# A decoder on one core: query and key biases as columns in ScalarE's copies, and a new order of GpSimd's work at the heads of both attention runs

## The chip, the cores and the metric

One core of a Trainium2 chip runs the whole program. The metric is the time of one execution in microseconds, the median of several. Five engines work beside each other in it: TensorE (PE in the profile; its weight loads are PEld), VectorE (DVE), ScalarE (ACT), GpSimd (POOL) and SyncE (SP), which here only issues DMAs. Each runs its own list of instructions in order and waits on semaphores.

## The reference, cut to what matters

The input x is four batches (B = 4) of 256 rows of 128 numbers. It passes through two layers of a decoder. Layer 0 is self-attention with random features (16 heads of width 8), cross-attention with a second input ctx, and a routed feed-forward part; layer 1 is causal self-attention, cross-attention and a feed-forward part with product keys. Each attention starts with a layer norm. What the change touches are the projections of layer 0:

```python
q = layernorm(x) @ Wq.T + bq        # layer 0, self-attention: stage 0
k = layernorm(x) @ Wk.T + bk
v = layernorm(x) @ Wv.T + bv
qh = split_heads(q @ wq.T + bq)     # layer 0, cross-attention: stage 1, q from x, k and v from ctx
kh = split_heads(k @ wk.T + bk)
vh = split_heads(v @ wv.T + bv)
```

The causal attention of layer 1 (stage 2) has no biases, and its cross-attention (stage 3) has one only on the output.

## The kernel before, in words

A turn n is one batch of one stage: n = 0 to 3 are stage 0, 4 to 7 stage 1, 8 to 11 stage 2, 12 to 15 stage 3. For every turn `norm` (L885, VectorE) takes the moments of two tiles of 128 rows, GpSimd raises the variance to the power of -0.5 (`power`, L472), and VectorE scales (L904). TensorE then turns the result (`pre_x`, L1326), ScalarE copies it out (`evac_x`), TensorE multiplies by the query and key weights (`pre_qk`, L1308) and by the value weights (`pre_v`), and ScalarE copies these out (`evac_qk`, L663, one instruction for queries and keys together, and `evac_v`). The queries and keys lie with features on partitions, so that a bias is one number for each partition.

The biases are added on TensorE: `project` follows a product by one whose contraction has only three rows (L1313 for queries and keys, L1314 for the rest). The three rows are the bias split into three bf16 parts, which VectorE makes in `split_bias` (L259 to L273): for 512 columns ahead of the first product, and for the other 640 in three pieces at the end of the steps n = 0, 1, 2 of stage 0's loop.

Stage 0 has two loops: one over the four turns that makes features (L972 on VectorE), and one that combines keys and values and ends a turn with `onorm_rf`, `tail_b`, `resid`, and `norm` and `pre` of turns 4 and 5 (L1025). After it stages 1, and later 2 with 3, are run by `run(first, last)`, a list that each engine has for itself: `run(4, 7)` and `run(8, 15)`. A run has a head: scores by rows for all 16 heads of the first turn, whose maxima VectorE takes (L943; L940 and L941 in stage 2), `max_parts`, `max_turn` (L1457), three early score products of the next turn, and then a loop of scores by columns (L1429, behind L1425 in stage 2), exponentials (L705) and values. The places of the later turns' `pre_x`, `pre_qk` and `pre_v` in that loop come from `pres_at`. In the head `norm(first + 2)` stands between `max_parts` and the early row maxima, and its `pre_x` and `pre_qk` stand behind the first two of the loop's score products.

For each turn of a run GpSimd splits the queries and keys into three bf16 parts (`split`, L484 to L500), and SyncE places them by 12 DMAs (`place`, L412) into one of three stacks, which GpSimd must have cleared (`clear`, L517, a memset of 128 by 4096). Ahead of `place` stands `fixed`, which waits for that clear.

Between the two runs lies the routed feed-forward part: 32 leaves, each with rows gathered by GpSimd's DMAs, 16 dot products on VectorE (`hidden`, L1130, both inputs in SBUF), 16 scalings on ScalarE (L817, after L807) and 34 products on TensorE (L1685). `add_leaf` (L1139) adds the leaves 24 to 31 to x. Its last steps also do `norm` and `pre` of the turns 8 and 9: VECTOR_AT, TENSOR_AT and SCALAR_AT name the leaf before which each stands. On GpSimd turn 8's power stands behind the gathers of leaf 30 and turn 9's behind those of leaf 31; then come `split(8)`, `clear(2)`, `split(9)`, `clear(0)`, `clear(1)` and the power of turn 10. The stacks share their memory with the leaves' rings, so the clears wait for the leaves.

## Time and profile before

| | us |
|---|---|
| median of 3 runs | 813.09 (812.82 to 814.02) |
| profiled execution | 818.24 |
| its span | 816.5 |
| stage 0 | 0 to 115 |
| run of stage 1 | 115 to 220 |
| routed feed-forward part | 220 to 450 |
| runs of stages 2 and 3 | 450 to 620 |
| product keys | 620 to 816 |

The stages are read from the order of the instructions in the timeline; their borders are rounded. A line of the timeline gives the start and the duration in us, the engine, the source line and the operation, what it writes and reads, and in brackets how long the engine had been idle and what ended that.

### The profile page before, as it was taken

Reading aid. Unit: us, or ns where it says so; the run is one execution under the profiler, and the core shown is the slowest. Engines: PE = TensorE matmul, PEld = TensorE weight load, DVE = VectorE, ACT = ScalarE, POOL = GpSimd, SP = SyncE. Lnnn points to the kernel's source line nnn. Section 1 sums busy time; section 2 is a strip of 40 time slices with the busy share of each in tenths; the row PEclk is TensorE's granted clock in tenths of the full one; section 3 lists DMA queues with packets and bytes.
Section 4 is the critical chain, followed back from the end, with each engine's and each line's share of the span. In section 5 each row is a group of like instructions: output and inputs, shape, how many; then the busy total and the mean of one; then the engine's idle time right before and its main releaser. Section 6 shows DMA issues by size and latency. Waiting matters only on the chain. (4 is left out here: it accounts for less than half of the span.)

```text
span 816.5 us, 14593 instructions
## 1 busy us (share of the span) xinstructions
PE 678.3 (83%) x4864; PEld 513.5 (63%) x4864; DVE 598.5 (73%) x2443; ACT 440.3 (54%) x1054; POOL 320.7 (39%) x315
## 2 busy tenths in 40 slices
PE   3987987978767989989879379989987698888888
PEld 1556634535346677878769256665545488888888
DVE  5695556774468999998758277787735699999984
ACT  1224002646227887879988035556664665555562
POOL 3050052460143423233213622223001688888883
PEclk9985555989859999989999689999999899999999
DMA  7000020200088999999634212112000000000000
GB/s 241 2 1 3 1 80 16 58 14 2 1 328 312 358 366 386 346 357 413 235 134 183 72 37 59 44 43 58 26 3 0 1 2 5 4 4 5 5 4 7
DMA packets 38914, 86.07 MB, mean 105 GB/s; under 512 B 3985, under 2 KB 30129, under 8 KB 30647
## 3 DMA queue, kind: packets, MB, share of 16 engines
q0 software_dynamic: 9216, 69.47, 21.8%
q1 hardware_dynamic: 29622, 15.66, 6.7%
q8 instruction: 39, 0.64, 0.3%
q14 instruction: 37, 0.30, 0.1%
HBM read 74.42 MB, written 0.52 MB: 92 GB/s over the span
## 5 line engine op out<-in xcount | busy, mean ns | idle before, releaser
L817 ACT ACTIVATE arena<-arena,hact 128x128 f32<-128x128 f32 x512 | 155.5, 388 | 1.0
L705 ACT ACTIVATE arena<-psum 128x512 f32<-128x512 f32 (+1 forms) x192 | 101.5, 561 | 56.5 <-PE psum L1429 55.9
L606 POOL TENSOR_TENSOR arena<-arena 128x1024 f32<-128x1024 f32 x64 | 121.2, 1913 | 21.9 <-DVE arena L1269 16.4
L1130 DVE CUSTOM_DVE_ANT_0 arena<-arena,fx 128x128 f32<-128x128 f32 x384 | 106.1, 344 | 10.4 <-DMA arena<-tab_q,leaf_no 8.5
L863 ACT ACTIVATE psum<-arena,tneg 128x1024 f32<-128x1024 f32 x64 | 71.5, 1118 | 61.8 <-DVE arena L1269 29.1
L1793 PE MATMUL psum<-arena 128*128 128x128 f32 x688 | 91.1, 294 | 16.3 <-DVE arena L1269 10.0
L943 DVE TENSOR_REDUCE rowmax<-psum 128x2 f32<-128x512 f32 x128 | 81.5, 686 | 26.1 <-PE psum L1411 24.5
L1793 PEld LDWEIGHTS psum<-arena 128*128 128x128 f32 x688 | 87.6, 209 | 18.4 <-DVE arena L1269 11.1
L1685 PE MATMUL psum<-identf,arena 128*128 128x128 f32 x544 | 78.5, 301 | 16.0 <-ACT arena L817 15.2
L1685 PEld LDWEIGHTS psum<-identf,arena 128*128 128x128 f32 x544 | 71.3, 210 | 23.3 <-ACT arena L817 16.5
L1411 PE MATMUL psum<-arena 128*128 128x256 bf16 (+1 forms) x384 | 77.3, 296 | 10.2 <-DVE rowmax L943 9.6
L1685 PE MATMUL psum<-arena,identf 128*128 128x128 f32 x544 | 73.3, 288 | 5.1 <-ACT arena L817 4.6
L1685 PEld LDWEIGHTS psum<-arena,identf 128*128 128x128 f32 x544 | 67.1, 199 | 11.0 <-ACT arena L817 5.0
L1429 PE MATMUL psum<-arena 128*128 128x256 bf16 (+1 forms) x384 | 69.2, 275 | 4.0 <-DMA arena<-mt 2.4
L1269 DVE SCALAR_TENSOR_TENSOR arena<-arena,vaug,psum 128x1024 f32<-128x1024 f32 x43 | 54.5, 1273 | 15.2 <-ACT psum L863 13.0
L475 POOL TENSOR_TENSOR rstd<-var_e,halves 128x2 f32<-128x2 f32 x16 | 11.3, 705 | 130.6 <-DVE var_e L899 130.6
L1411 PEld LDWEIGHTS psum<-arena 128*128 128x128 bf16 x384 | 35.2, 105 | 32.4 <-DVE rowmax L943 26.5
L648 ACT ACTIVATE arena<-psum 128x128 f32<-128x128 f32 (+3 forms) x57 | 29.3, 514 | 47.0 <-PE psum L1445 10.4
L1445 PE MATMUL psum<-arena,vaug 128*32 128x256 f32 (+1 forms) x768 | 49.2, 375 | 1.9 <-ACT arena L705 1.9
L1429 PEld LDWEIGHTS psum<-arena 128*128 128x128 bf16 x384 | 33.7, 100 | 25.8 <-ACT arena L705 13.7
L1793 PE MATMUL psum<-arena,picked 128*128 128x128 f32 x336 | 44.6, 289 | 6.1 <-DVE picked L1269 6.1
L1793 PEld LDWEIGHTS psum<-arena,picked 128*128 128x128 f32 x336 | 42.3, 204 | 7.2 <-DVE picked L1269 7.1
(230 smaller groups left out, 1202.4 us busy)
## 6 DMA issues: line engine op xcount, KB each, us to landing
arena<-parts SPq DMA_DIRECT2D x144, 64.0 KB
w_sb<-attn_w SPq DMA_DIRECT2D x1, 768.0 KB, 7.9
x<-x_in SPq DMA_DIRECT2D x1, 512.0 KB, 4.1
fx<-ctx_in SPq DMA_DIRECT2D x1, 512.0 KB, 4.6
picked<-mask_in SPq DMA_DIRECT2D x1, 512.0 KB, 6.2
wq_sb<-peer_wq SPq DMA_DIRECT2D x1, 512.0 KB, 8.3
down_sb<-table_down SPq DMA_DIRECT2D x1, 512.0 KB, 9.5
up_sb<-table_up SPq DMA_DIRECT2D x1, 512.0 KB, 8.9
```

Source lines behind the costliest of these rows:

```text
L606: nc.gpsimd.tensor_tensor(grid[k % 3].rearrange("p (i j) -> p i j", i=PK), sim[:, t, h, :].unsqueeze(2).to_broadcast([P, PK, PK]), sim[:, ...
L705: nc.scalar.activation(probs[k % (2 * HG)][:, 0:w], bank(2 + k % 2, 0, w), ACT.Exp, scale=float(D) ** -0.5).then_inc(probs_ready, 1)
L817: a = nc.scalar.activation(w, w, ACT.Copy, scale=hact[i % 2][:, l:l + 1])
L863: nc.scalar.activation(psum[:, (4 + 2 * (k % 2)) * BANK:(6 + 2 * (k % 2)) * BANK], grid[k % 3], ACT.Exp, bias=tneg[:, t, h:h + 1]).then_in ...
L943: i = nc.vector.tensor_reduce(rowmax[n % 2][:, :, h], bank(k % 2).rearrange("p (s n) -> p s n", s=SUB), AX.X, ALU.max)
L1130: i = nc.vector.tensor_tensor_reduce(w, w, src, 1.0, r[:, LW * E + l:LW * E + l + 1], ALU.mult, ALU.add, hid[g % 4][:, l:l + 1])
L1269: nc.vector.scalar_tensor_tensor(out=picked[k % 3], in0=grid[k % 3], scalar=top[t][:, h, TOPK - 1:TOPK], in1=psum[:, (4 + 2 * (k % 2)) * B ...
L1411: i = nc.tensor.matmul(o[:, r:r + keys], q[:, s * P:s * P + P], kk[:, 0:keys], start=not causal, stop=True, skip_group_check=causal)
L1429: i = nc.tensor.matmul(bank(2 + k % 2, c * S, c * S + S - q0), kk[:, c * P:c * P + P], q[:, q0:S], start=not causal, stop=True, skip_group ...
L1445: i = nc.tensor.matmul(o, vaug[n % 4][:, c, g * HG + j, :], probs[(k + j) % (2 * HG)][:, c * S:c * S + S - q0], start=(c == 0), stop=(c == ...
L1685: i = nc.tensor.matmul(o, *ab, start=(l == 0), stop=(l == LW and f < 3))
L1793: i = nc.tensor.matmul(psum[:, o:o + P], picked[k % 3][:, c * P:c * P + P], diag[t % 2][:, h, :], start=(h == 0 and c % 4 == 0), stop=(h = ...
```

## The change: what it does

The query and key biases of stages 0 and 1 come in as a tile of 9 rows by 128 by one more DMA, are turned into columns by one TensorE transpose, and are copied out by two small ScalarE instructions. `evac_qk` then is two instructions in these stages, each with function Identity and a bias column; there are no three-row products for queries and keys, and `split_bias` makes 640 of 1152 columns. In the head of a run `norm(first + 2)` is done before the run (in stage 0's second loop, and behind the last leaf), and its `pre_x` and `pre_qk` stand ahead of the first score product by columns. On GpSimd `power(6)` stands ahead of `split(5)`; at the second head `split(8)` no longer waits behind turn 9's power, turn 9's and 10's powers stand behind `clear(2)`, and `split(9)` stands last.

```diff
         bias_p = sb("bias_p", [3, NB], bf16)
+        bias_c = sb("bias_c", [P, 6])
         nodes_sb = sb("nodes_sb", [P, 4, NODES])
...
+        bias_r = arena[0:9, 2048:2048 + P]
         bias_sb, bias_w = arena[0:3, 0:9 * P], arena[0:3, 9 * P:9 * P + 9 * P // 2].bitcast(bf16)
...
         nbias_ready = sem("nbias_ready")
+        bias_ps, columns_ready = sem("bias_ps"), sem("columns_ready")
         bias_ready, osb_ready, or_ps = sem("bias_ready"), sem("osb_ready"), sem("or_ps")
...
-            now = [("x", n + 2)] * (n in (B, 2 * B) and h == 0) + [("qk", n + 2)] * (n in (B, 2 * B) and h == 1)
-            now += [("v", n + 2)] * (h == 2) + [("x", n + 3)] * (h == H - 2) + [("qk", n + 3)] * (h == H - 1)
+            now = [("v", n + 2)] * (h == 2) + [("x", n + 3)] * (h == H - 2) + [("qk", n + 3)] * (h == H - 1)
             return [(what, m) for what, m in now if m <= last]
...
                      ("weigh", 2): 24, ("attend", 2): 25, ("route_f", 2): 25, ("weigh", 3): 27, ("attend", 3): 28,
-                     ("route_f", 3): 29, ("next", NEXT[0]): 29, ("next", NEXT[1]): 32}
+                     ("route_f", 3): 29, ("next", NEXT[0]): 29, ("moments", NEXT[1]): 31, ("scale", NEXT[1]): 32,
+                     ("next", NEXT[1] + 1): 32}
...
             sp.dma_start(w_sb[:, 0:4, :], attn_w[0:4].rearrange("a i o -> i a o")).then_inc(in_w, 16)
+            sp.dma_start(bias_r, attn_bias.rearrange("(a p) -> a p", p=P)).then_inc(in_w, 16)
             sp.dma_start(bias_sb, attn_bias.partition_broadcast(3)).then_inc(in_w, 16)
...
                                                  bass.IndirectOffsetOnAxis(no, 0)).then_inc(rows2_in[g % RING2], 16)
-                    if g >= len(ORDER) - SUB:
-                        power(NEXT[g - len(ORDER)])
+                    if g == len(ORDER) - SUB:
+                        power(NEXT[0])
                 split(NEXT[0])
...
                 clear(NEXT[0] % 3)
-                split(NEXT[1])
+                power(NEXT[1])
+                power(NEXT[1] + 1)
                 pool.wait_ge(leaf_done, len(ORDER) - 1)
...
                 clear((NEXT[1] + 1) % 3)
-                power(NEXT[1] + 1)
+                split(NEXT[1])
...
             clear(0)
+            power(B + 2)
             split(B + 1)
-            power(B + 2)
             run(*RUNS[0])
...
                     act.wait_ge(dd_ps, min(n - 1, B))
-                scale = float(D) ** -0.25 if stage(n) == 0 else 1.0
-                nc.scalar.activation(qk_f[n % 2][:, :, :], bank(5).rearrange("p (w n) -> p w n", w=2),
-                                     ACT.Copy, scale=scale).then_inc(qk_ready, 1)
+                if stage(n) < 2:
+                    act.wait_ge(columns_ready, 1)
+                    for w in range(2):
+                        i = nc.scalar.activation(qk_f[n % 2][:, w, :], bank(5, w * S, w * S + S), ACT.Identity,
+                                                 bias=bias_c[:, 4 * stage(n) + w:4 * stage(n) + w + 1],
+                                                 scale=float(D) ** -0.25 if stage(n) == 0 else 1.0)
+                    i.then_inc(qk_ready, 1)
+                else:
+                    copy(qk_f[n % 2][:, :, :], bank(5).rearrange("p (w n) -> p w n", w=2), qk_ready)
...
+            act.wait_ge(bias_ps, 1)
+            nc.scalar.activation(bias_c[:, 0:2], bank(6, 0, 2), ACT.Copy, scale=float(D) ** -0.25)
+            copy(bias_c[:, 4:6], bank(6, 4, 6), columns_ready)
             evac_x(0)
...
                 evac_mt(first)
+                evac_x(first + 2)
+                evac_qk(first + 2)
                 for n in range(first, last + 1):
...
-            def norm(n):
+            def moments_of(n):
...
                 nc.vector.tensor_scalar(var_e[:, :], mv[:, :, 1], 1e-5, None, ALU.add).then_inc(var_ready, 1)
+
+            def norm_scale(n):
+
+                b = batch(n)
                 dve.wait_ge(rstd_ready, n + 1)
...
                 dve.wait_ge(xn_ready, n + 1)
+
+            def norm(n):
+                moments_of(n)
+                norm_scale(n)
...
             dve.wait_ge(consts, 1)
-            dve.wait_ge(in_w, 48)
-            split_bias(nc.vector, link, 0, 4 * P)
-            nc.vector.tensor_copy(bias_w[:, 0:1], bias_p[:, 0:1]).then_inc(bias_ready, 1)
+            dve.wait_ge(in_w, 64)
+            split_bias(nc.vector, link, 2 * P, 4 * P)
+            nc.vector.tensor_copy(bias_w[:, 0:1], bias_p[:, 2 * P:2 * P + 1]).then_inc(bias_ready, 1)
             nc.vector.tensor_tensor(feat_w[:, :, :], head16[:, :].unsqueeze(2).to_broadcast([P, H, M]),
...
                 dve.wait_ge(zk_ready, n + 1)
-                if n < B - 1:
+                if 0 < n < B - 1:
                     split_bias(nc.vector, link, (4 + 2 * n) * P, min(6 + 2 * n, 9) * P)
-            nc.vector.tensor_copy(bias_w[:, 0:1], bias_p[:, 0:1]).then_inc(bias_ready, 1)
+            nc.vector.tensor_copy(bias_w[:, 0:1], bias_p[:, 2 * P:2 * P + 1]).then_inc(bias_ready, 1)
             link(nc.vector.tensor_reduce(kmax1[:, :], kmax[:, :], AX.X, ALU.max))
...
                     resid(n - 1)
-                if 1 <= n < B - 1:
+                if n >= 1:
                     norm(B + n - 1)
...
                 max_parts(first)
-                norm(first + 2)
                 for h in range(EARLY):
...
                             add_leaf(i - 2)
+                    elif what == "moments":
+                        moments_of(i)
+                    elif what == "scale":
+                        norm_scale(i)
                     elif what == "norm":
...
-            BIAS = {(0, 0): 0, (0, 1): 1, (0, 2): 2, (0, 3): 3, (1, 0): 4, (1, 1): 5, (1, 2): 6, (1, 3): 7, (3, 3): 8}
-
-            def project(o, lhs, rhs, key, by_row):
+            BIAS = {(0, 2): 2, (0, 3): 3, (1, 2): 6, (1, 3): 7, (3, 3): 8}
+
+            def project(o, lhs, rhs, key):
...
                 bias = bias_of(r * P, r * P + P)
-                if by_row:
-                    return nc.tensor.matmul(o, bias, ones[0:3, :], start=False, stop=True)
                 return nc.tensor.matmul(o, ones[0:3, 0:P], bias, start=False, stop=True)
...
                 for w, src in ((0, xn_t[n % 2][:, :]), (1, kv_of(n))):
-                    i = project(bank(5, w * S, w * S + S), w_sb[:, 4 * a + w, :], src, (a, w), True)
+                    i = project(bank(5, w * S, w * S + S), w_sb[:, 4 * a + w, :], src, (a, w))
                 i.then_inc(qk_ps, 1)
...
                     i = project(bank(4, S + s * P, S + s * P + P), kv[:, s * P:s * P + P], w_sb[:, 4 * a + 2, :],
-                                (a, 2), False)
+                                (a, 2))
                 i.then_inc(v_ps, 1)
...
                     i = project(bank(tail_bank(n) + 1, s * P, s * P + P), o[:, s * P:s * P + P], w_sb[:, 4 * stage(n) + 3, :],
-                                (stage(n), 3), False)
+                                (stage(n), 3))
                 i.then_inc(y_ps, 1)
...
             pe.wait_ge(consts, 1)
-            pe.wait_ge(in_w, 48)
+            pe.wait_ge(in_w, 64)
+            nc.tensor.transpose(bank(6, 0, 9), bias_r, identf[0:9, 0:9]).then_inc(bias_ps, 1)
             pre_x(0)
+            pre_qk(0)
             pe.wait_ge(bias_ready, 1)
-            pre_qk(0)
             pre_v(0)
...
                 max_turn(first)
+                pre_x(first + 2)
                 for h in range(EARLY):
                     score_rows(first + 1, h)
+                pre_qk(first + 2)
                 for n in range(first, last + 1):
```

## Rows read from the trace of the kernel before

**Rows 1.** The page's first part: engine, busy us, share of the span, instructions.
```profile
PE 678.3 (83%) x4864; PEld 513.5 (63%) x4864; DVE 598.5 (73%) x2443; ACT 440.3 (54%) x1054; POOL 320.7 (39%) x315
```

**Rows 2.** The timeline of the first 20 us: bias split, first projections, first features.
```profile
9.65 0.41 DVE L262 CAST arena<-arena 3x512 bf16<-3x512 f32 x1
...
14.60 1.22 PE L1308 MATMUL psum<-xn_t,w_sb 128*128 128x256 f32 x2 [4.18 <-DVE arena L969]
...
15.75 0.39 PE L1313 MATMUL psum<-ones,bias_p 3*128 3x256 bf16 x1
...
17.66 0.60 ACT L663 ACTIVATE qk_f<-psum 128x512 f32<-128x512 f32 x1 [6.81 <-PE psum L1313]
...
19.43 3.78 PE L1476 MATMUL psum<-feat_w,qk_f 128*128 128x512 f32 x4
```

**Rows 3.** ScalarE's groups by shape: busy us, mean ns of one, idle before.
```profile
L648 ACT ACTIVATE vaug<-psum 128x256 f32<-128x256 f32 x16 | 6.1, 384 | 13.9 <-PE psum L1314 9.2 <-PE psum L1308 4.8
```

**Rows 4.** The timeline of stage 0's first loop.
```profile
28.79 0.70 PE L1308 MATMUL psum<-xn_t,w_sb 128*128 128x256 f32 x2 [0.47 <-ACT xn_t L648]
...
31.25 1.04 POOL L482 TENSOR_TENSOR sq<-qk_f 128x512 f32<-128x512 f32 x1 [11.22 <-ACT qk_f L663]
...
31.38 1.19 DVE L265 TENSOR_TENSOR arena<-arena 3x256 f32<-3x256 f32 x1
...
33.42 0.41 DVE L265 TENSOR_TENSOR arena<-arena 3x256 f32<-3x256 f32 x1
...
48.09 0.60 DVE L904 TENSOR_SCALAR xn<-x,mv,rstd 128x128 f32<-128x128 f32 x2 [0.81 <-POOL rstd L475]
...
48.74 0.44 PE L1326 MATMUL psum<-identf,xn 128*128 128x128 f32 x2 [2.00 <-DVE xn L904]
```

**Rows 5.** The timeline at the end of the third turn of that loop.
```profile
54.84 7.06 DVE L266 CAST arena<-arena 3x128 bf16<-3x128 f32 x1
54.86 6.96 POOL L517 MEMSET arena<- 128x4096 f32 x2
...
63.39 1.23 DVE L982 TENSOR_REDUCE stab<-psum 128x32 f32<-128x1024 f32 x1
```

**Rows 6.** The timeline of stage 0's end and the first head.
```profile
98.94 0.39 PE L1313 MATMUL psum<-ones,bias_p 3*128 3x256 bf16 x1
...
127.79 0.41 PE L1457 MATMUL psum<-identb,mparts 128*48 128x128 bf16 x2 [1.88 <-DVE mparts L957]
...
131.68 0.64 PE L1429 MATMUL psum<-arena 128*128 128x256 bf16 x2
...
137.03 0.61 PE L1429 MATMUL psum<-arena 128*128 128x256 bf16 x2
```

**Rows 7.** The timeline from the last leaves to the second head.
```profile
431.57 5.08 PE L1685 MATMUL psum<-arena,identf 128*128 128x128 f32 x34
...
432.93 0.22 ACT L807 ACTIVATE hact<-hid 128x16 f32<-128x16 f32 x1 [0.72 <-DVE hid L1130]
...
443.48 0.72 POOL L475 TENSOR_TENSOR rstd<-var_e,halves 128x2 f32<-128x2 f32 x1 [13.33 <-DVE var_e L899]
444.18 0.60 POOL L495 CAST parts<-qk_f 128x512 bf16<-128x512 f32 x1
444.24 1.86 DVE L904 TENSOR_SCALAR xn<-x,mv,rstd 128x128 f32<-128x128 f32 x2 [0.84 <-POOL rstd L475]
...
455.80 6.96 POOL L517 MEMSET arena<- 128x4096 f32 x2
...
462.57 0.39 PE L1406 MATMUL psum<-causal_q,identb 128*128 128x256 bf16 x1 [10.83 <-DMA arena<-parts]
```

**Rows 8.** The timeline in the second head: ScalarE's table load.
```profile
475.30 1.28 ACT L705 ACT_TABLE_LOAD   x1
```

**Rows 9.** Busy us of each engine in two stretches, with TensorE's granted clock.
```profile
28.00:48.00 20.00, 17.36 (x77) 9.82 (x75) 17.20 (x39) 7.01 (x12) 3.41 (x4) 1.00 0.00 1
72.00:90.00 18.00, 18.00 (x100) 15.19 (x98) 8.51 (x14) 5.28 (x7) 0.00 (x0) 0.50 0.02 4
```

## The prediction

> **What bounds the kernel now.** I read the page first. No engine is full: TensorE is the busiest with 83% of the span [rows 1], so time is lost where one engine waits for another, and a change pays only at such places. The chain of waits reaches back only to the product keys and shows nothing of the three places that are changed, so I went through the timeline at each of them. In the first 20 us TensorE stands idle for 4.18 us until VectorE has split the biases; its first projection starts at 14.60 [rows 2]. In stage 0's first loop VectorE is as full as TensorE, and TensorE waits 2.00 us for turn 3's norm [rows 4]. At the end of the third turn a cast of VectorE takes 7.06 us and ends right behind two memsets of GpSimd (54.86 + 6.96 = 61.82), and the next row maximum starts only at 63.39 [rows 5]. At the second head TensorE is idle for 10.83 us until the parts of turn 8 lie in the stack [rows 7]. Everything behind such a place is carried by semaphores and would move with it.
>
> **Part A, the first projections.** TensorE no longer waits for the split. The scaled x is read out by about 10.9; I add 0.2 for the transpose of the bias tile and the two small copies in front of it. The first product then starts at 11.1 instead of 14.60. Each bias product lengthens its pair: from 14.60 to the next pair behind 15.75 lie 1.47 us where the pair itself takes 1.22, so 0.25 each at this speed [rows 2]. Queries and keys: 11.1 + 2 x 1.22 = 13.5. The values take the 1.9 us from the release of ScalarE's copy, 0.1 ahead of 17.66, to 19.43 [rows 2], and end at 15.4, if their own bias is there by 13.5. It is: the split begins at 9.65 as before, is half as wide, and its nine operations take some 3.4 us at the width of 256. The features start at 15.4 instead of 19.43: **-4.0**. ScalarE's copy becomes two of 256 columns, 0.38 each by the nearest row [rows 3] against 0.60 for one, so 0.16 more (up to 0.4, as a bias column may cost something); the features wait for the value products anyway, which covers it. The DMA of 4.6 KB is one more issue of 0.4 us in front of the others; if its landing is late, A loses up to 0.5.
>
> **Part B, stage 0's first loop.** VectorE's split behind turn 0 goes, some 3.9 us with the operation that takes 1.19 instead of 0.41 beside GpSimd's squares [rows 4]. So far it sat in front of turn 2's norm and turn 1's maximum. Followed step by step with durations of this trace, turn 2's scaling ends at about 29.4, the features of turn 1 at 29.3 (the maximum follows them, not the norm), turn 1's last subtraction at 35, the split of the next 256 columns at 39, turn 3's norm at 41.8. Before, that norm ended at 48.69 [rows 4]: -6.9, of which A gave 4.0. TensorE is through with turn 1's work by 41.8 as well, so its wait of 2.00 us goes and nothing takes its place. What is late next is the cast beside the memsets. Both chains, the split of 128 columns on VectorE and the clears on GpSimd, start from turn 3's norm: the clears came 6.8 us behind its start, the blocked cast at the same time [rows 4, 5]. After the change the one chain loses two bias products (0.28 at this speed) and gains 0.16 on ScalarE, the other loses nothing. So I let the stall stay, and it ends when the clears do, 6.8 earlier. A and B together: **-6.8**, between -4.8 (TensorE reaches its full speed only at the same absolute time as before, near 28, and 4 us of its work take twice as long) and -13.4 (the stall goes, a rival below).
>
> **Part C, stage 0's end.** TensorE works without a gap from 72 to 90 at half clock [rows 9] and nearly so to 115. Two turns lose two bias products each at 0.25: **-1.0** (0 to -1.3, with 0.32 by [rows 6] for the whole step). Turn 6's norm moves here, 1.3 us of moments and 0.6 of scaling on VectorE. It is hidden in VectorE's idle time of 7.1 us ahead of the last residual; GpSimd's power for it stands behind `clear(0)` and ahead of `split(5)`, which has about 1.5 us of idle time in front of it. Without that cover `split(5)` would be late by 0.7, and its DMAs have 10 us of row maxima before they are needed.
>
> **Part D, the first head.** Between `max_turn` (127.79) and the third score product by columns (137.03) lie 9.24 us [rows 6]. In the new order: 0.34 for `max_turn`, 0.55 for `pre_x`, 1.05 for two early products, then the third, which waits for a row maximum that is no longer behind the norm (until 2.8), two projections of 1.22 (5.3), two pairs of products as before (7.5). **-1.8**, of which 0.5 are bias products. The first product by columns comes later than before (5.3 against 3.89), so ScalarE starts later but then isn't interrupted; if that counts, D is +1.4, if nothing counts, 0. I take -1.7. Turn 7, in the loop, loses two bias products at 0.14: **-0.3**.
>
> **Part E, the second head.** GpSimd was held at turn 9's power until 443.48; `split(8)` followed at 444.18, and `clear(2)`, which SyncE needs ahead of its 12 DMAs, only then [rows 7]. Now `split(8)` runs at 431.6, when turn 8's projections are out, and the clear at 436.8, when TensorE is through with leaf 28 (431.57 + 5.08) [rows 7]. SyncE's 8 us of DMAs are over by 452, and TensorE's wait of 10.83 us would go. Three things are late in its place.
> First, `split(8)` reads SBUF for 3.5 us (0.60 + 1.16 + 0.61 + 1.16) while VectorE makes `hidden(29)`, for which ScalarE already waits 0.72 us [rows 7]. A VectorE operation with two SBUF inputs took 1.19 instead of 0.41 beside GpSimd [rows 4]. I take the same for `hidden`, though no row shows it: +3.5 on the leaves (0 to 3.5).
> Second, turn 9's moments ahead of `hidden(31)` are 1.4 us on VectorE, against a slack of 0.8: +0.7. The last leaf ends at 453.5 instead of 449.3, and TensorE is through with turn 9 at 456.1.
> Third, turn 10's scaling. It waits for a power behind which GpSimd starts `clear(0)` and `clear(1)` at once, 6.96 us [rows 7]. GpSimd won that race before: power, cast at 444.18, and the scaling took 1.86 instead of 0.60 [rows 4, 7]; and a cast waited through both memsets [rows 5]. So the scaling waits from 450 to 457, then beside `split(9)` to 458.8, and behind it on VectorE stand the last two `add_leaf` and all row maxima of turn 8. TensorE gets two heads further and waits. The maxima start at 459.3 instead of 463.3: **-4.0**. `split(9)` is late (457), but its DMAs are placed by 467, and turn 9's first scores are wanted at 471. In the head itself the order of part D is worth less, since ScalarE's table load of 1.28 [rows 8] was hidden behind the DMA of the maxima and now follows `evac_qk`: **-0.3** (+1 to -1.6). Bounds of E: -10.8 with neither block, -0.4 if `hidden` also waits 3.5 for `clear(2)`, a memset (and +0.6 with the worst of the head).
> The Trainium skill, SBUF — State Buffer, Who interferes with whom, speaks on that last bound: a VectorE instruction with two SBUF inputs contends with a GpSimd instruction that reads SBUF and not with one that only writes. By it the split blocks `hidden` and the memset doesn't, which is E as summed; E would be near nothing if it weren't so. No row of this trace has such an instruction beside a memset.
>
> **The sum.** -6.8 - 1.0 - 1.7 - 0.3 - 4.3 = -14.1. The profiled execution of 818.24 would become 804.1. The median of the runs is 5.15 lower, a difference that the change doesn't touch: 813.09 - 14.1 = **799.0**.
>
> **The rivals.**
> 1. The stall at the clears goes. It needs VectorE's last split (2.4 us) to be over before GpSimd's clears start, so that TensorE must be 1.5 us late behind turn 3's norm. Turn 3's maximum then comes 6.9 earlier, but the reduction over partitions waits for the clears: -6.6 more, 792.4. For it: the two chains meet within 0.02 us in the trace [rows 5]. Against it: both hang on one norm.
> 2. `hidden` isn't blocked by the split: the last leaf ends 3.5 earlier, and so do norm and clears: 799.0 - 3.6 = 795.4. For it: no row shows `hidden` blocked. Against it: its two inputs.
> 3. The second head gives nothing, because VectorE's blocks (split, clear and scaling) fill the 10.83 us: 799.0 + 4.3 = 803.3.
> 4. TensorE doesn't get its full clock in the first loop. For it: from 72 to 90 it is busy all the time and has 0.50 granted [rows 9]. In 20 us from 28 it is busy 17.36 at 1.00; at the speed of the prologue's pairs (1.22 us against 0.70 [rows 2, 4]) that is 12 more, and B's 2.8 go too: 799.0 + 14.8 = 813.8, no change within what can be measured.
> 5. Slower: Identity isn't in the table set that Exp uses. ScalarE then loads tables ahead of each of the eight changed `evac_qk` and again ahead of the next Exp: 16 x 1.28 = 20.5 [rows 8], all of it between a projection and what waits for it or in front of the exponentials, so 799.0 + 20.5 = 819.5. It decides from 11 loads on the path. Against it: Copy stands among the Exps without a load. The Trainium skill, ScalarE: Activation LUTs, Table sets: the hidden batching unit, counts identity among the functions that are in every set; by it this rival falls.
> A change that does nothing is not among them: the wait for the split is taken away in the code.
>
> **How the numbers follow.** The forecast 52%, its own range 795 to 803; rival 1 14%, rival 2 13%, rival 3 11%, rival 4 4%, rival 5 6%. The range takes in rivals 1 to 3 with some of their sums and leaves out 4 and 5: 789 to 808. Faster by over 0.2% (1.6 us, about what a measurement of this kernel can tell from no change): the first four, with little taken off, 0.88. Within 0.2%: 0.04. Slower: 0.08.
>
> **What would show it.** A: L1308 first at 11.1, L1476 first at 15.4. B: turn 3's L904 at 41.2 and no wait of TensorE behind it; the L266 of about 7 us still there, and L982 at 56.6. D: 7.5 us from `max_turn` to the third L1429. E: L495 of turn 8 near 422 (431.6 less A to D), L1130 with gaps of 0.6 and 1.2 beside it, L904 of turn 10 as long as two memsets, L1406 without a wait for the DMA. The prediction is wrong if ScalarE's table loads are more than seven, if the granted clock of the first 50 us differs, or if the leaves take longer by more than 5 us.

## The result, and the profile after

| | before | after |
|---|---|---|
| median of the runs | 813.10 (812.82 to 814.02) | 788.34 (785.38 to 789.27) |
| profiled execution | 818.24 | 788.61 |
| its span | 816.5 | 786.9 |

The ratio is 0.9687 (95% interval 0.966 to 0.9714): 24.8 us less. The forecast was 799.0, in a range of 789 to 808. The sign was right, the gain was 10.7 us larger than forecast, and the median lies 0.7 us below the range.

The first two parts of the page of after, to be read beside [rows 1]. TensorE has 16 us less busy time: the products are hardly fewer, but fewer of them run at half clock.

```profile
PE 662.3 (84%) x4849; PEld 506.1 (64%) x4849; DVE 603.8 (77%) x2434; ACT 442.1 (56%) x1064; POOL 321.1 (41%) x315
...
PEclk9985559898568999999999999999999899999999
```

The timeline of after from the first projection on [rows 2]. The four projection products are one unbroken group of 2.07 us, and turn 0's features start at 14.99 instead of 19.43. The half norms behind them take 1.01, and the next four products of the features 1.96.

```profile
10.82 2.07 PE L1335 MATMUL psum<-xn_t,w_sb 128*128 128x256 f32 x4 [0.47 <-ACT xn_t L653]
13.11 0.80 PE L1335 MATMUL psum<-w_sb,xn_t 128*128 128x128 f32 x2 [0.22 <-DVE arena L993]
14.99 3.78 PE L1502 MATMUL psum<-feat_w,qk_f 128*128 128x512 f32 x4
18.57 1.01 PE L1513 MATMUL psum<-half,sq 128*128 128x16 f32 x8
19.43 1.96 PE L1502 MATMUL psum<-feat_w,qk_f 128*128 128x512 f32 x4
```

The end of the third turn of after, GpSimd's row first [rows 5]. The two memsets still hold VectorE's casts, but as two waits of 3.26 and 2.81 with two operations between them, and turn 3's row maximum (L1006, before L982) follows at 52.19 instead of 63.39.

```profile
44.52 7.04 POOL L521 MEMSET arena<- 128x4096 f32 x2
...
44.84 3.26 DVE L269 CAST arena<-arena 3x128 bf16<-3x128 f32 x1
48.13 0.34 DVE L273 SCALAR_TENSOR_TENSOR bias_p<-arena,identf,bias_p 3x128 bf16<-3x128 bf16 x1
48.51 0.28 DVE L268 TENSOR_TENSOR arena<-arena 3x128 f32<-3x128 f32 x1
48.82 2.81 DVE L269 CAST arena<-arena 3x128 bf16<-3x128 f32 x1
...
52.19 1.23 DVE L1006 TENSOR_REDUCE stab<-psum 128x32 f32<-128x1024 f32 x1
```

The projections of turn 4 in after, at half clock [rows 6]. Without the bias products, queries, keys and values start 1.01 and 0.86 us apart; before, it was 1.47 and 1.48.

```profile
86.58 1.22 PE L1335 MATMUL psum<-xn_t,w_sb 128*128 128x256 f32 x2 [0.47 <-ACT xn_t L653]
87.59 1.06 PE L1335 MATMUL psum<-ctx_t,w_sb 128*128 128x256 f32 x2
88.45 0.63 PE L1335 MATMUL psum<-w_sb,ctx_t 128*128 128x128 f32 x2
```

The second head of after: GpSimd, VectorE (L1153 is `hidden`, L924 turn 10's scaling, L964 the first row maximum of turn 8), then TensorE [rows 7]. `split(8)` lengthens four dot products, the memset behind it none (0.35). Turn 10's scaling lasts as long as two memsets. TensorE starts its scores by rows at 435.70 without a wait for the DMA.

```profile
413.26 0.71 POOL L499 CAST parts<-qk_f 128x512 bf16<-128x512 f32 x1 [1.95 <-ACT qk_f L653]
414.05 1.15 POOL L501 TENSOR_TENSOR resid_f<-qk_f,parts 128x512 f32<-128x512 f32 x1
...
418.21 3.52 POOL L521 MEMSET arena<- 128x4096 f32 x1 [1.09 <-PE psum L1715]
...
429.62 6.96 POOL L521 MEMSET arena<- 128x4096 f32 x2
```

```profile
413.42 0.69 DVE L1153 CUSTOM_DVE_ANT_0 arena<-arena 128x128 f32<-128x128 f32 x1
...
414.05 1.31 DVE L1153 CUSTOM_DVE_ANT_0 arena<-arena 128x128 f32<-128x128 f32 x1
...
418.57 0.35 DVE L1153 CUSTOM_DVE_ANT_0 arena<-arena 128x128 f32<-128x128 f32 x1
...
429.71 7.02 DVE L924 TENSOR_SCALAR xn<-x,mv,rstd 128x128 f32<-128x128 f32 x2 [0.81 <-POOL rstd L479]
...
437.16 0.28 DVE L964 TENSOR_REDUCE rowmax<-psum 128x1 f32<-128x128 f32 x1
```

```profile
435.70 0.27 PE L1431 MATMUL psum<-causal_q,identb 128*128 128x256 bf16 x1
```

### The profile page after: what moved, and what is told of

Same layout as the page of the kernel before. It is cut to its first block and busy times, and to the rows that moved or that the text cites. A ratio compares the mean times of both kernels' runs of the same rounds, so it can differ in the third digit from the quotient of the medians.

```text
span 786.9 us, 14564 instructions
## 1 busy us (share of the span) xinstructions
PE 662.3 (84%) x4849; PEld 506.1 (64%) x4849; DVE 603.8 (77%) x2434; ACT 442.1 (56%) x1064; POOL 321.1 (41%) x315
## 5 line engine op out<-in xcount | busy, mean ns | idle before, releaser
L1153 DVE CUSTOM_DVE_ANT_0 arena<-arena,fx 128x128 f32<-128x128 f32 x384 | 106.1, 347 | 7.8 <-DMA arena<-tab_q,leaf_no 6.9
L1436 PE MATMUL psum<-arena 128*128 128x256 bf16 (+1 forms) x384 | 73.2, 282 | 9.5 <-DVE rowmax L967 8.0
L1713 PEld LDWEIGHTS psum<-arena,identf 128*128 128x128 f32 x544 | 65.4, 193 | 13.5 <-issue 6.3
L1454 PE MATMUL psum<-arena 128*128 128x256 bf16 (+1 forms) x384 | 67.2, 269 | 4.3 <-DMA arena<-mt 2.6
L1436 PEld LDWEIGHTS psum<-arena 128*128 128x128 bf16 x384 | 33.2, 101 | 30.6 <-DVE rowmax L967 26.2
L1454 PEld LDWEIGHTS psum<-arena 128*128 128x128 bf16 x384 | 33.2, 99 | 25.7 <-ACT arena L716 13.3
L1821 PEld LDWEIGHTS psum<-arena,picked 128*128 128x128 f32 x336 | 42.3, 204 | 7.2 <-DVE picked L1296 7.1
```

Of the source, the lines that this page charges most:

```text
L1153: i = nc.vector.tensor_tensor_reduce(w, w, src, 1.0, r[:, LW * E + l:LW * E + l + 1], ALU.mult, ALU.add, hid[g % 4][:, l:l + 1])
L1436: i = nc.tensor.matmul(o[:, r:r + keys], q[:, s * P:s * P + P], kk[:, 0:keys], start=not causal, stop=True, skip_group_check=causal)
L1454: i = nc.tensor.matmul(bank(2 + k % 2, c * S, c * S + S - q0), kk[:, c * P:c * P + P], q[:, q0:S], start=not causal, stop=True, skip_group ...
L1713: i = nc.tensor.matmul(o, *ab, start=(l == 0), stop=(l == LW and f < 3))
L1821: i = nc.tensor.matmul(psum[:, o:o + P], picked[k % 3][:, c * P:c * P + P], diag[t % 2][:, h, :], start=(h == 0 and c % 4 == 0), stop=(h = ...
```

## The experiments

Twelve runs were made in three groups of four, each group on a chip of its own, with the kernel before timed beside it. Below, a median is followed by the lowest and the highest run, and a ratio (to the kernel before of the same group) by its 95% interval. To compare the traces I read ten points in each and took the stretch between neighbours. "Turn 3" is the start of its row maximum (L982); "stage 0" the last residual of stage 0 (L932); "parts n" the start of the last operation of `max_parts(n)` (L957); "leaf 26" its `add_leaf`; "maxima 8" the first row maximum of turn 8; "end" the span.

| kernel | turn 3 | stage 0 | parts 4 | parts 5 | parts 7 | leaf 26 | maxima 8 | parts 8 | parts 9 | parts 15 | end |
|---|---|---|---|---|---|---|---|---|---|---|---|
| before | 63.39 | 50.94 | 13.21 | 20.87 | 42.43 | 228.05 | 44.43 | 11.01 | 16.65 | 104.32 | 221.20 |
| before again | 61.81 | 50.94 | 13.21 | 17.50 | 42.55 | 227.65 | 44.97 | 11.82 | 16.57 | 104.18 | 221.20 |
| bias only | 54.26 | 48.47 | 13.63 | 17.82 | 42.09 | 228.29 | 44.83 | 11.55 | 17.58 | 103.85 | 221.63 |
| order only | 61.19 | 51.01 | 13.21 | 18.15 | 42.42 | 224.90 | 37.08 | 10.22 | 15.38 | 104.21 | 220.23 |
| second head old | 52.49 | 48.55 | 13.40 | 15.53 | 42.06 | 225.11 | 44.84 | 10.99 | 16.34 | 104.05 | 221.24 |
| after | 52.19 | 48.55 | 13.36 | 16.61 | 41.78 | 227.56 | 37.11 | 10.22 | 15.37 | 103.87 | 220.28 |
| after again | 54.52 | 48.54 | 13.54 | 16.37 | 42.32 | 226.27 | 37.09 | 10.20 | 15.37 | 103.87 | 220.21 |
| one split | 44.86 | 54.70 | 13.62 | 16.02 | 42.09 | 227.48 | 37.07 | 10.95 | 15.23 | 103.85 | 220.83 |
| late clears | 51.84 | 48.55 | 13.35 | 16.60 | 41.60 | 227.47 | 36.12 | 10.20 | 15.78 | 103.82 | 221.17 |
| all three | 44.84 | 54.45 | 13.39 | 16.23 | 36.77 | 226.46 | 36.11 | 10.21 | 15.50 | 103.83 | 221.61 |
| products kept | 53.40 | 51.00 | 13.23 | 18.15 | 42.68 | 228.59 | 37.18 | 10.22 | 15.38 | 103.89 | 220.18 |
| wait back | 55.47 | 48.55 | 13.35 | 15.48 | 42.11 | 225.46 | 37.12 | 10.22 | 15.39 | 103.88 | 220.17 |
| early products | 51.33 | 48.57 | 13.42 | 16.61 | 41.60 | 230.35 | 37.33 | 10.21 | 15.37 | 103.88 | 221.03 |
| all and early | 47.76 | 50.58 | 13.41 | 16.40 | 36.77 | 231.36 | 36.34 | 10.21 | 16.01 | 103.91 | 221.15 |

Most columns repeat to 0.1 us between kernels that share the code there. Four don't: turn 3, parts 5 and the end, which follow the speed of TensorE (below), and leaf 26, the gathers, where kernels with the same code differ by up to 3 us and the two with early products lie another 2 to 3 higher.

### The kernel before, once more

> The kernel before, unchanged, for a second profile. Its first profile lies 5 us above its other runs, and the change moved the profiled execution by 29.6 us but the median by 24.8. Theory 1 (TensorE's clock in the first loop differs from execution to execution): this profile shows another time at which the pairs of L1308 become short (28.8 in the first profile), and turn 3's maximum (L982, 63.39 before) moves with it by some us, the whole by as much. Theory 2 (profiling costs these 5 us wherever it is done): the starts up to 120 us are as in the first profile within 0.3.

814.11 us, beside 815.16 (810.08 to 819.78) of the group. Against the profile of before, turn 3 comes 1.6 earlier and parts 5 another 3.4. The starts differ by far more than 0.3, so it isn't profiling that costs this. The one profiled execution that I had worked from held 5.0 us up to parts 5 that another execution of the same kernel doesn't have; 0.9 of them are made up later.

### Bias only, order only

The first takes the columns and the smaller split and leaves the order of both heads as before (two of its pieces, against the changed kernel):

```diff
-                power(NEXT[1])
-                power(NEXT[1] + 1)
+                split(NEXT[1])
                 pool.wait_ge(leaf_done, len(ORDER) - 1)
                 clear(NEXT[1] % 3)
                 clear((NEXT[1] + 1) % 3)
-                split(NEXT[1])
+                power(NEXT[1] + 1)
...
-                pre_x(first + 2)
                 for h in range(EARLY):
                     score_rows(first + 1, h)
-                pre_qk(first + 2)
```

> Only the bias columns, no new order at either head. Theory 1 (the parts are separate and the semaphores carry each to the end): about 11.2 us by the start of stage 0's second loop, 2 more by the first head, little after: 800 to 802 by the median, as some of the 11.2 is the first profile's own excess. Theory 2 (my sizes were right and the rest of the gain comes from the heads): 813.1 - 8.1 = 805.

The second is the converse: the kernel before with the new order.

> Only the new order at both heads, the biases by products as before. Theory 1: the first head gives 2 to 4 us and the second 9.8, as read between the two profiles: 799 to 801. Theory 2 (the second head gives the 4.3 that I forecast): 806 to 808. If the two parts need each other, the gains of this run and of the bias columns alone don't add to 24.8.

Bias only took 803.96 (803.54 to 805.70), 0.9857 (0.9794 to 0.9919), 11.2 less than before; order only 801.58 (799.71 to 804.82), 0.9842 (0.9776 to 0.9909), 13.6 less. Their sum is 24.8, the whole change; with intervals of 5 us each way that it comes out to the tenth is luck. Bias only gains all it gains by stage 0: turn 3 and the 48.47. Its median lies between my two theories. Order only shows no gain at the first head (parts 5 is 18.15 against 17.50 and 20.87) and gains 10.5 to 11.6 behind leaf 26; another 3 us of this trace are its short stretch of gathers (224.90).

### The second head as before

The whole change, but the second head in its old order (one piece of the edit):

```diff
-                evac_x(first + 2)
-                evac_qk(first + 2)
+                if first == B:
+                    evac_x(first + 2)
+                    evac_qk(first + 2)
```

> The changed kernel with the second head as it was (GpSimd's order behind the last leaves, turn 9's and 10's norms, turn 10's projections). Theory 1: it loses the 9.8 us that the milestones show between leaf 28 and turn 9's maxima: 788.3 + 9.8 = 798.1. Theory 2 (4.3 as forecast): 792.6.

802.20 (796.36 to 804.05), 0.9844 (0.978 to 0.9909): 13.0 less than before, so by the medians the second head is worth what is missing to 22 to 25, 9 to 12; by the table 10.6: 7.7 up to the maxima, 0.8 to parts 8, 1.0 to parts 9, 0.2 and 1.0 behind (the last 1.0 isn't the head's, see E below). TensorE's wait is back in its timeline:

```profile
441.23 0.40 PE L1433 MATMUL psum<-causal_q,identb 128*128 128x256 bf16 x1 [11.26 <-DMA arena<-parts]
```

### The changed kernel, once more

> The changed kernel itself, so that the others of this group stand against it on one chip. Theory (the second head's wait for the DMA is gone whole, and the row maxima start 3.8 us behind the last leaf instead of 14.1): median 24 to 26 us below the kernel before; from the end of the last leaf to the first row maximum of turn 8 3.8 us; from max_parts(8) to max_parts(9) 15.4. Rival (part of the gain was the granted clock of one execution or one chip): under 22 us, and TensorE's full speed later than at 19 us.

790.83 (788.12 to 791.93) beside 812.97 (810.61 to 818.23): 0.9717 (0.9668 to 0.9766), 22.1 less, and not the 24 to 26 that I expected; 15.37 between the parts 8 and 9 came as expected. The change is worth 22 to 25 us. In this execution TensorE's rows run at half speed until 23 us (the four products of 3.66 below), against 18.6 in the first trace of after, and turn 3 comes 2.3 later. The timeline of this run; compare the half norms, 1.73 here and 1.01 there:

```profile
18.57 1.73 PE L1513 MATMUL psum<-half,sq 128*128 128x16 f32 x8
20.13 3.66 PE L1502 MATMUL psum<-feat_w,qk_f 128*128 128x512 f32 x4
23.63 0.38 PE L1351 MATMUL psum<-identf,xn 128*128 128x128 f32 x2
```

### No cast beside the clears

```diff
-                if 0 < n < B - 1:
-                    split_bias(nc.vector, link, (4 + 2 * n) * P, min(6 + 2 * n, 9) * P)
+                if n == 1:
+                    split_bias(nc.vector, link, 6 * P, 9 * P)
```

> Only edit: the three pieces of bias that VectorE splits behind the turns 1, 2 and 3 are split in one go behind turn 1, so that no cast of VectorE stands beside GpSimd's two clears. Theory (the cast is held by the memsets, and turn 3's maximum behind it, at 52.19): that maximum comes some 6 us earlier, near 45.5; the reduction over partitions behind it waits for the clears, which end at 51.6, so the kernel gains 0 to 2 us more than turn 3's maximum is worth to TensorE: 5 to 7 us below the changed kernel. Rival 1 (what counts is the end of the clears, not the cast): 0 to 1 us. Rival 2 (TensorE's idle time behind the cast is what brings its granted clock down to 0.50 at 52 us until 121): the clock stays 1.00 in the second loop and the kernel gains 15 us and more.

787.45 (784.76 to 793.27), 0.9687 (0.9622 to 0.9753), 3.4 less than after in this group, short of the 5 to 7 of the theory, and the spread doesn't tell it from nothing. The stall is gone: turn 3 at 44.86. But stage 0 gives most of it back (54.70 against 48.55). From turn 3's scaling (38.12 in after, 39.00 here) to the end of stage 0 lie 62.62 and 60.56: 2.1 us gained. Nor did the clock stay up: 0.50 from 60 to 80 here too. The wait has moved to GpSimd's reduction over partitions (L526), which here starts 6.02 us behind the end of the clears (45.39 + 6.96 = 52.35) though its input was ready from 50.9 on; the idle time is put down to "issue", that is to no releaser. What the trace does show is two MODIFY_POOL_CONFIG of the reduction's line on GpSimd's sequencer, directly behind the clears. The two other kernels with one split, where the input is early too, have them at 52.27 and 53.19 and the reduction at 58.09 and 58.77, 5.8 and 5.6 us behind. In after it starts 6.40 behind the clears (51.56), and only there does its input come last. So the reduction comes at 58.37 instead of 57.96, and TensorE waits for it 5.74 us instead of for VectorE. GpSimd's rows of this kernel, the first from the view of line L526, and TensorE's:

```profile
L526 POOLq MODIFY_POOL_CONFIG  x2: 18/18/18, 52.3 to 52.3; - x2
58.37 0.38 POOL L526 PARTITION_ALL_REDUCE kmaxg<-kmax  x1 [6.02 <-issue]
```

```profile
60.90 1.50 PE L1573 MATMUL psum<-vaug,arena 128*128 128x36 f32 x6 [5.74 <-DVE arena L1032]
```

### The clears behind turn 10's scaling

```diff
                 pool.wait_ge(leaf_done, len(ORDER) - 1)
+                pool.wait_ge(xn_ready, NEXT[1] + 2)
                 clear(NEXT[1] % 3)
```

> Only edit: at the second head GpSimd starts its two clears when turn 10's scaling is done. Theory (the scaling waits 7.02 us for both memsets, but TensorE's first row products of turn 8 come out at 436.0 only, 0.8 before the maxima can start): 0.5 to 1.2 us less than the changed kernel, the scaling back at 0.60 us and the maxima right behind TensorE's products. Rival (the block is what held the last part of the second head, as the prediction had it): 4 us less. Second rival (nothing, as the clears and turn 9's split come later): 0 to 0.5 more.

787.13 (785.45 to 792.18), 0.9684 (0.9625 to 0.9744), 3.7 less than after in the group. The scaling takes 0.60 again. The maxima come 0.97 sooner behind leaf 26 (36.12 against 37.09) and not 4, so the block held next to nothing; parts 9 (+0.4) and the end (+1.0) take it back, and the lower median isn't explained by it; the spreads overlap. The trace also prices the leaves, since both last `add_leaf` stand free: the last is at 432.99, 33.58 behind leaf 26's, against 30.62 before.

```profile
429.05 0.60 DVE L925 TENSOR_SCALAR xn<-x,mv,rstd 128x128 f32<-128x128 f32 x2 [0.81 <-POOL rstd L479]
...
432.99 0.29 DVE L1163 TENSOR_TENSOR x<-x,psum 128x128 f32<-128x128 f32 x1 [3.01 <-PE psum L1716]
435.53 0.29 DVE L965 TENSOR_REDUCE rowmax<-psum 128x1 f32<-128x128 f32 x1 [2.25 <-PE psum L1437]
```

### All three

Both edits above and one more, ahead of GpSimd's split of the node bias:

```diff
             pool.wait_ge(in_tab, 32)
+            pool.wait_ge(mparts_ready, 3)
             p = bias_p[:, 9 * P:NB]
```

> Three edits together: the one split, the late clears, and GpSimd's split of the node bias kept back until VectorE has made the max_parts of turn 6. Theory (the three VectorE blocks add up; max_parts of the turns 5 and 6 lose 5.5 us beside GpSimd's operations): 10 to 13 us less than the changed kernel. Rival 1 (the blocks are hidden behind TensorE and the gathers): 2 to 5 us. Rival 2 (the clock of the second loop stays at 1.00): over 20 us.

782.81 (781.17 to 785.80), 0.9634 (0.9585 to 0.9683), 8.0 less than after in the same group, between rival 1 and the theory. The third edit is the one that pays: parts 7 comes 36.77 behind parts 5 instead of 41.6 to 42.3. The last row of `max_parts(6)`, of after and then of this kernel:

```profile
154.05 1.06 DVE L981 TENSOR_TENSOR mparts<-remax,mparts 128x32 bf16<-128x32 f32 x1
```

```profile
147.14 0.19 DVE L983 TENSOR_TENSOR mparts<-remax,mparts 128x32 bf16<-128x32 f32 x1
```

### The three-row products kept

```diff
+                    if a < 2 and n > 0:
+                        nc.tensor.matmul(o, w_sb[:, 4 * a + w, :], src, start=True, stop=False)
+                        i = nc.tensor.matmul(o, bias_of(2 * P, 3 * P), ones[0:3, :], start=False, stop=True)
```

> Only edit: the turns 1 to 7 keep a three-row product behind each query and key projection, with three rows of the split that a later piece of the program fills as well, beside the columns (the output is then not the reference's). Theory (behind a pair the next pair starts 0.46 us later instead of 0.25 at half clock): from turn 3's row maximum to the last residual of the first stage 50.9 us instead of 48.5, the turns 2 and 3 0.3 to 0.5 later, turn 7 0.3 later: 3 to 4 us slower than the changed kernel. Rival (each product costs 0.25 at half clock and 0.14 at full, as the prediction had it): 1.5 to 2 us slower.

795.25 (790.95 to 795.93), 0.9768 (0.9729 to 0.9806), 17.9 below before instead of 22 to 25: 4 to 7 slower than after in the groups on the other chips, which is the theory or more and not the rival. Stage 0 is back at 51.00, and parts 5 at 18.15, the value of order only. The first loop, at full clock, pays too: in turn 1 queries, keys and values start at 22.07, 22.91 and 23.75, in after at 22.08, 22.62 and 23.05, so the two products cost 0.7 there. The pitch of 1.47 is back:

```profile
87.79 1.22 PE L1371 MATMUL psum<-xn_t,w_sb 128*128 128x256 f32 x2 [0.47 <-ACT xn_t L653]
88.94 0.39 PE L1372 MATMUL psum<-ones,bias_p 3*128 3x256 bf16 x1
89.26 1.22 PE L1371 MATMUL psum<-ctx_t,w_sb 128*128 128x256 f32 x2
```

### The wait for the split, put back

```diff
-            split_bias(nc.vector, link, 2 * P, 4 * P)
+            split_bias(nc.vector, link, 0, 4 * P)
...
             pre_x(0)
-            pre_qk(0)
             pe.wait_ge(bias_ready, 1)
+            pre_qk(0)
             pre_v(0)
```

> Only edit: VectorE splits all four pieces of turn 0's bias again and TensorE waits for them ahead of its first projection. Theory (TensorE's full speed comes a fixed stretch behind the start of its work, so the late start is paid in full): features of turn 0 at 19.2 to 19.4 instead of 14.99, turn 3's row maximum 4.2 to 4.6 later, 4 to 5 us slower than the changed kernel. Rival (full speed comes at a fixed time of the program, so that an early start is spent at the slow one): 2 us slower or less.

792.23 (788.99 to 794.51), 0.9756 (0.9726 to 0.9787), 20.9 below before. The features start at 18.16, 3.17 later: less than I expected, as the values' bias is ready by then. Turn 3 comes at 55.47, 1.0 and 3.3 behind the two traces of after, and the median lies 1.2 to 3.9 behind, so the wait was worth 3.2 us at the features and 1 to 4 in all. TensorE's rows become fast between 21.7 and 22.9 here, within the times that two executions of after already span, so the run doesn't decide between the theory and its rival.

```profile
14.58 2.07 PE L1335 MATMUL psum<-xn_t,w_sb 128*128 128x256 f32 x4 [4.23 <-DVE arena L993]
...
18.16 3.78 PE L1502 MATMUL psum<-feat_w,qk_f 128*128 128x512 f32 x4
21.73 1.18 PE L1513 MATMUL psum<-half,sq 128*128 128x16 f32 x8
```

### Products ahead of the first work

```diff
+            pe.wait_ge(pool_step, 3)
+            for _ in range(14):
+                nc.tensor.matmul(bank(7, 256, 384), identf[:, :], identf[:, :], start=True, stop=True)
             pe.wait_ge(consts, 1)
...
+            for _ in range(2):
+                nc.tensor.matmul(bank(7, 256, 384), identf[:, :], identf[:, :], start=True, stop=True)
             pre_x(0)
```

> Only edit: ahead of its first work, from 3.5 to 9.6 us, TensorE makes 16 products of the identity matrix into a bank that nobody reads. Theory (its rows run at half speed until some 8 to 11 us of nearly unbroken work are behind it, though the granted clock is 1.00): the first pairs take 0.7 instead of 1.22 us, turn 0's features 1.96 instead of 3.78, and turn 3's row maximum comes 3.5 to 5 earlier: 3 to 5 us less than the changed kernel. Rival (VectorE holds the first loop as much as TensorE): turn 0 is faster, but turn 3's row maximum only 1 to 2 us earlier, 1 to 2 us less in all. Second rival: no effect on the speed, 0.

787.19 (785.77 to 791.45), 0.9679 (0.9649 to 0.9709): 25.9 below before, 1 to 4 more than after in the groups on the other chips. The first four projection products took 1.13 instead of 2.07, but the granted clock then fell to 0.76 and 0.81 between 12 and 20 us, where after has 1.00, and the features took 3.50. Turn 3 came at 51.33, 0.5 ahead of the earliest with the same stage 0 and without them. Windows of this run (length; busy time and instructions of PE, PEld, DVE, ACT and POOL; granted clock; DMA share; GB/s):

```profile
12.00:16.00 4.00, 2.86 (x8) 1.62 (x9) 3.28 (x10) 0.98 (x3) 1.53 (x2) 0.76 1.01 359
16.00:20.00 4.00, 4.00 (x15) 2.19 (x14) 2.51 (x5) 0.00 (x0) 0.31 (x1) 0.81 0.62 158
```

The last kernel puts the same products ahead of all three edits.

> The early products together with the one split, the late clears and the node bias kept back. Theory: the sum of its parts, 8.0 (measured for the three) plus 3 to 5: 11 to 13 us less than the changed kernel, 33 to 36 less than the kernel before. Rival (the earlier clears and the rest of stage 0 take it back): 8 to 9 less than the changed kernel.

779.52 (775.12 to 785.66), 0.9573 (0.9535 to 0.961): 33.6 below before, the fastest kernel of the study; without the early products it was 30.2 below on another chip, so by the medians they add 3.4, within the spread of either. Its trace doesn't show that gain at turn 3, which comes at 47.76 instead of 44.84: the granted clock is 0.50 from 44 to 52 us here and 1.00 in all three. Stage 0 then takes 50.58 instead of 54.45, so 1.0 us is left at its end.

## Why the prediction was wrong, point by point

| step | forecast | measured |
|---|---|---|
| A, features of turn 0 | -4.0 | -4.4 |
| A and B, turn 3 | -6.8 | -8.9 to -9.4 |
| C, stage 0 | -1.0 | -2.4 |
| D, parts 4 to 5 | -1.7 | -1.0 |
| turn 7 | -0.3 | -0.2 to -0.8 |
| E, behind leaf 26 | -4.3 | -10.3 |
| sum | -14.1 | -23 to -24 |

A and B stand in pairs of traces whose half norms took about as long: 63.39 and 54.52 with 1.73, 61.19 (order only) and 51.84 (late clears) with 0.96; 61.81 (before again) and 52.49 (second head old) with 1.31 and 1.35 lie between. Before itself differs by 3.4 between its two executions up to parts 5, so D is not known better than that. D is against the 17.50 of before again, E after against before.

**A** was right in mechanism; 0.4 more came from C's error.

**B** was right in what stalls and what doesn't. The turn 3 scaling came 7.6 earlier in the pair of 1.73 (48.09 and 40.46), 7.7 and 8.0 in the others, not 6.9. The clears then start 6.4 us behind that scaling in after, against 6.8 in before and 8.1 in before again and order only; the prediction changed that distance by only 0.1. Part of this is the bias products, which C mis-sized: with them kept it is 7.4. In before, moreover, five more operations of the split stood behind the cast, 1.49 us up to the maximum; in after three of them, the second cast among them, had started before the memsets ended, and 0.56 is left behind that cast. In before again and order only the tail is as short (0.56 and 0.25), so this part isn't the change's. Rival 1, that the stall goes, did not happen, though its 792.4 lies nearer to the measured time than the forecast does, and its price was wrong too: with the stall taken away, 2.1 us came instead of 6.6, since the reduction over partitions does not follow the clears at once but 6 us behind them.

**C** mis-sized the bias product. I took the 1.22 us of the row of a pair for what a pair costs alone, and so 0.25 for the product. A row's duration isn't its pitch: without the product the next pair starts 1.01 or 0.86 us behind. Each product cost 0.46 to 0.62; two turns give 2 x (2.95 - 1.87) = 2.2 of the 2.4. The kept products show it: 51.00 against 48.54.

**D** can't be told apart from when TensorE gets its full clock at this head. Counted from `max_turn(4)` the granted clock is up after 16 us in before (parts 5: 20.87), after 10 in order only and products kept (18.15 each), after 9 in bias only (17.82), after 7 in before again (17.50) and after 3.5 to 6.7 with the whole change (15.5 to 16.6). The rows give one part of the gain: in the kernel that keeps the products the two pairs stand 1.32 and 1.47 apart at this place, in after 0.86 and 0.85, so 1.1. That the order gives anything by itself isn't shown. Windows of before, then of after (length; TensorE's busy time and instructions; granted clock; DMA share; GB/s):

```profile
132.00:136.00 4.00, 4.00 (x16) 0.50 0.04 7
136.00:140.00 4.00, 4.00 (x15) 0.50 0.00 0
140.00:144.00 4.00, 4.00 (x23) 0.53 0.32 88
```

```profile
116.00:120.00 4.00, 3.57 (x14) 0.50 0.11 20
120.00:124.00 4.00, 3.75 (x24) 0.87 0.13 33
```

Why it differs between two executions of one kernel stays open. That difference is also most of what the profiled execution of before had over its own median, 5.15; the prediction called it a difference that the change doesn't touch, but the changed kernel's profiled execution lies 0.3 above its median and has nothing of it.

**E** is the step that failed: -4.3 against -10.3, 6.0 of the 9 to 10 us missed. It has three terms, each mis-sized.
- The leaves were forecast 4.2 later and are 2.96 later (33.58 against 30.62). `split(8)` lengthened four dot products by 2.5 in sum (0.69 + 1.31 + 0.54 + 1.31 against four of 0.35), of which 1.3 show in the step from leaf 26 to 27 (15.24 against 13.92); the moments cost 1.2 each at the next two. So rival 2 (`hidden` isn't blocked) was wrong. The bound with the memset was wrong too: beside it `hidden` kept its 0.35. The Trainium skill, SBUF — State Buffer, Who interferes with whom, says just this of a two-input instruction beside a GpSimd instruction that only writes; the trace agrees.
- Behind the last leaf I had the maxima 5.8 later, against 14.07 before (463.32 - 449.25); they came 3.79 later (437.16 - 433.37). The scaling was blocked as forecast, 7.02, but I added 1.8 for `split(9)` beside it. That split can only start when both memsets are through, and the scaling is through then too (436.53). And the block is hidden: without it the maxima came only 0.97 sooner, since TensorE's first scores come at 435.70 anyway.
```profile
456.00:462.00 6.00, 0.00 (x0) 0.50 0.38 107
462.00:466.00 4.00, 3.06 (x16) 0.50 0.26 64
```

```profile
430.00:436.00 6.00, 5.51 (x42) 1.00 0.21 50
436.00:440.00 4.00, 2.21 (x17) 1.00 0.16 39
```

The kernel with one split shows what this costs. Its second head is that of after, but its clock falls during the same maxima, and its parts 8 is 10.95 instead of 10.22, nearly the 11.01 of before:

```profile
440.00:442.00 2.00, 1.75 (x10) 0.50 0.41 103
```

So the 0.8 is the clock. For the 1.3 up to parts 9 no run tells the clock from the norm and projections of turn 10 that moved away. The 0.9 behind parts 15 is the clock as well, but not this wait's: 6 us behind parts 15 it falls to half in before and not in after, and it falls in early products too, whose second head is that of after and whose end is 221.03. Windows of before, of after and of early products:

```profile
601.00:603.00 2.00, 2.00 (x20) 0.54 0.00 0
```

```profile
572.00:574.00 2.00, 1.63 (x21) 1.00 0.00 0
```

```profile
574.00:576.00 2.00, 2.00 (x18) 0.50 0.00 0
```

The same fall stands in before again, second head old, late clears, and all and early, all with 221.1 to 221.3 at the end. Bias only, one split and all three don't have it but a longer one further on, about 6 us instead of 3 to 4, from 20 us behind parts 15 (221.6, 220.8 and 221.6). So this 0.9 belongs to the measured gain, but that it came with the new head is luck; E by its own mechanism is -9.4. The bound of -0.4 that the prediction gave for a memset that blocks `hidden` is also off by its own terms, -4.3 + 3.5 = -0.8.

The terms of the table sum to 23 to 24; the medians say 24.8 and 22.1. Rivals 3 (the second head gives nothing) and 4 (no full clock in the first loop) are refuted by E's row and by the 1.96 us features at 19.43 in after. Rival 5 is refuted by the ScalarE rows: no table load stands at the first projections, and the second head's one load (452.41, 1.28) is the one of before, moved.

## What to carry to other kernels

Price an instruction that stands between two others by the start-to-start distance with and without it, never by the duration of a row: rows overlap, and the product that cost 0.25 by durations cost 0.46 to 0.62. When a long wait of TensorE goes, add what it runs behind the wait at half clock: here 1 to 2 of 10 us. And a block is worth only what the last of its waiters waits: of two 7 us blocks taken away, one gave 2.1 and one 1.0, while a handful of VectorE operations of 0.2 us, stretched beside GpSimd's split of the node bias, gave 5.

## What was unexpected of the hardware

TensorE's first rows ran at half speed though the profile gives a granted clock of 1.00 up to 48 us in before and in after: 1.73 for the half norms against 0.96 later. When they became fast differed between executions of one kernel (18.6 or 23 us in after), worth 2.3 us at turn 3. Early products made the start fast and the next 8 us slow (0.76 and 0.81 granted from 12 to 20 us).

A VectorE cast beside two memsets in a row waited for both (7.06 and 6.88, before and before again) or only for one (3.26 and 2.81, after), with other VectorE operations getting in between. It isn't the change that decides this: order only, with the stage 0 of before, waited once in a cast (3.43) and once in a scaling of the split (3.46). The scaling of turn 10 waited for both, 7.02, in all seven traces in which it stood there. What decides that stays open.

GpSimd's reduction over partitions came 6.0 us behind its last memset with its input ready (58.37, one split), behind two MODIFY_POOL_CONFIG of its own line. That these cause the 6 us is likely and not tested. If these 6 us could be had under the clears' start, most of the stall would be worth taking away; that wasn't tried.

Each ScalarE copy of 256 columns with a bias column took 0.47 where a plain one takes 0.38 [rows 3]; two in a row overlap and took 0.84, 0.24 more than the one of 512 columns that they replace, and not the 0.16 of the forecast.
